# The seam between two programs of a sandwich network: spreads over four PSUM banks, first rows placed in SBUF, products without a reader

## The chip, the core and the metric

One core of a Trainium2 chip runs one program; the metric is its device time in microseconds (us). A core has five engines with instruction queues of their own: PE (TensorE: matrix products into PSUM banks), DVE (VectorE), ACT (ScalarE), POOL (GpSimd) and SP (SyncE, which here only issues transfers). They meet through semaphores alone. The kernel before was run three times: 1757.78, 1751.74 and 1754.74 us, median 1754.74.

## The reference, cut to what matters

```python
x = x + layernorm(attention(layernorm(x)))        # 32 batches x 256 steps x 128, 16 heads
x = x + layernorm(ternary_ffn(layernorm(x)))      # 128 -> 512 -> 512 -> 512 -> 128, two gelu layers
x = x + layernorm(rnn(layernorm(x)))              # h = tanh(x_t Wi + b + h Wh), over the steps, all batches at once
x = x + layernorm(shared(x') + routed(x'))        # x' = layernorm(x); one of 32 experts for each row
```

The attention works on one batch at a time. All that follows works on steps: the recurrence wants all 32 batches of a step together.

## The kernel before, in words

The program has two halves with a seam between them. `attention_layer` makes x1 = x + layernorm(attention) for each of the B = 32 batches and writes it to a tensor in DRAM, `x1_d`, ordered by step, then batch. `mixing_experts` reads `x1_d` in 16 chunks of 512 rows; chunk c holds steps 16c to 16c+15 of all batches. Each half is a block: a Python function per engine writes its instruction list by hand, a barrier of all engines ends the block, POOL clears the semaphores of that half, and the next block begins.

Attention is a pipeline over batches. `rounds` calls `step(b, f, n, m, z, y, par)` for b = -3 to 33: b is the batch whose scores are taken, z = b-1 the one whose output is finished, y = b-2 the one whose residual is made. The last two rounds have little left in them: round 32 finishes batch 31 (z) and makes the residual of batch 30 (y), round 33 makes the residual of batch 31. The chain of the finishing batch goes so:

- DVE `reciprocal` (L799 to L808) takes one over the softmax sums and splits it into `rec_parts`.
- PE `spread_out(z, g)` (L530), for g = 0 to 3, spreads a quarter of the reciprocals over the partitions: two products of 256 columns into the one PSUM bank `spread`. It waits until DVE has read the bank for g-1 (semaphore onT).
- DVE `normalise` (L817) multiplies four heads of `onT` by the bank; in the round of batch z, the statistics of batch y (L742, L746) stand between the third and the fourth.
- PE `output` (L544), eight pieces of two 128x128 products in full fp32, each pair of pieces after its `normalise`; ACT copies the result to `y_sb` (L734); DVE takes statistics (L742, L746), POOL the root (L354, L356), DVE normalises (L948) and adds the residual input `xr` into `x1` (L954).
- SP, per batch y: wait for x1 of y-1, load `xr` (L268); wait for x1 of y, store it to `x1_d` (L271). There is one buffer for each of `xr` and `x1`. At its end SP waits for all 32 stores.

`mixing_experts` begins with 15 small constants on POOL (L1190 to L1199); PE, ACT and DVE wait for all of them. SP loads chunk 0 of `x1_d` into `x1c` (L1148), DVE takes its statistics (L1736, L1740), POOL the roots (L1212, L1214), DVE normalises (L1745), PE turns the chunk (`turn4`, L1279), ACT and DVE split it, and four rounds of the first feed-forward layer follow: six products of 512 columns on PE (L1435 to L1438), tanh on ACT (L1663), two multiplications on DVE (L1944, L1950); each round of PE waits for the DVE of the round before. From the second chunk on PE has the second layer and later stages of earlier chunks to fill its waits.

`keep_busy` is already there in the end of this half: products of a weight with a weight, 128x512, into a bank nobody reads (L1351).

Of the kernel before, what the change touches and what calls it, by code (L numbers as in the profile page):

```python
# [14 lines left out]
P = 128  # L15
# [76 lines left out]

def attention_layer(nc, x, w_qk, w_v, w_rot, w_out, bonus0, bonus_step, x1_d, mix, mix_d, room, row_buf, sorted_d):

    with ExitStack() as ctx:
# [87 lines left out]
        yn = sb("yn", [P, TT, D])  # L183
        x1 = sb("x1", [P, TT, D])

# [24 lines left out]
        block = ctx.enter_context(nc.Block(no_gpsimd_drain=True))  # L210

        def rounds(eng, step):

            def row(b):
                return [v if 0 <= v < B else None for v in (b, b + 1, b + 2, b + 3, b - 1, b - 2)] + [b % 2]
            for b in range(-3, 3):
                step(*row(b))  # L220
            with eng.Fori(0, (B - 6) // 2) as i:
                for k in range(2):
                    b = 2 * i + (3 + k)
                    step(b, b + 1, b + 2, b + 3, b - 1, b - 2, 1 - k)
            for b in range(B - 3, B + 2):
                step(*row(b))

        @block.sync
        def _(sp):
# [22 lines left out]
            def step(b, f, n, m, z, y, par):  # L252
# [213 lines left out]
        def _(pe):  # L466
# [53 lines left out]
            def spread_out(z, g):  # L520
# [5 lines left out]
                if g == 0:  # L526
                    wait(pe, s["rec_parts"], z + 1)
                wait(pe, s["onT"], GROUPS * z + g)
                for i in range(2):
                    m = pe.matmul(spread[:, i, :], back_to_r[:, 2 * g + i].rearrange("p i d -> p (i d)"),  # L530
                                  rec_parts[:], start=True, stop=True)
                m.then_inc(s["p_bc"], 1)

            def output(z, par, pieces):
# [38 lines left out]
            def step(b, f, n, m, z, y, par):  # L573
# [26 lines left out]

                values(f, par, 1)
                spread_out(z, 0)
                if f is not None:
# [47 lines left out]

            rounds(pe, step)

        @block.scalar
        def _(act):
# [79 lines left out]

            rounds(act, step)

        @block.vector
        def _(dve):
# [71 lines left out]
            def normalise(z, par, g):  # L811
# [156 lines left out]

def mixing_experts(nc, early, x1_d, mix, wgu, row_buf, sorted_d, gate_up, down, sh_gate_up, sh_down, out):

# [5 lines left out]
    with ExitStack() as ctx:  # L976
# [105 lines left out]

        ctx.callback(clear, nc, list(s.values()))
        block = ctx.enter_context(nc.Block(no_gpsimd_drain=True))

        def rounds(eng, step, drain):
# [48 lines left out]
        def _(sp):  # L1135
# [140 lines left out]
        def _(pe):  # L1276
# [5 lines left out]
            def rnn_step(r, t):  # L1282
# [4 lines left out]
                          skip_group_check=True).then_inc(s["p_step"], 1)  # L1287

            pe.wait_ge(s["const"], N_CONST)

# [45 lines left out]
            def ranks(q, bank):  # L1336
# [10 lines left out]
                m_.then_inc(s["p_rank"], 1)  # L1347

            def keep_busy(n, bank):
                for _ in range(n):  # L1350
                    pe.matmul(bank[:, :], w1_part[0][:, 0:P], w1_part[0][:, :], start=True, stop=True)  # L1351

# [378 lines left out]
        def _(dve):  # L1731
# [156 lines left out]
            def step(p, a, c, v, h, q, z, par):  # L1888
# [29 lines left out]
                def first_norm():  # L1918
                    if p is not None:
                        wait(dve, s[f"xc{par}"], 8 * (p - par) + 16)  # L1920
                        stats("f", lambda k: x1c[:, k, :], p)

                if v is not None:
                    sums(v)
                if a is not None:
                    wait(dve, s["p_xn2T"], a)
                    apply("f", xn2, lambda k: x1c[:, k, :], "xn2", a)
                if v is not None:
# [106 lines left out]
def build(nc, t, out):  # L2035
# [6 lines left out]
    with ExitStack() as ctx:  # L2042
        def sb(name, shape, dt=F32):
            return ctx.enter_context(nc.sbuf_tensor(name, shape, dt))

        wgu = sb("wgu", [P, E, 2 * I])
        row_buf = [sb(f"row_buf{i}", [P, CT, ROW]) for i in range(3)]
        with ExitStack() as early:
            mix = mixing_weights(nc, ctx, early)
            attention_layer(nc, t["x"], t["w_qk"], t["w_v"], t["w_rot"], t["w_out"], t["bonus0"], t["bonus1"], x1_d,  # L2050
                            mix, t, wgu[:].rearrange("p e i -> p (e i)"), row_buf[0], sorted_d)
            mixing_experts(nc, early, x1_d, mix, wgu, row_buf, sorted_d, t["gate_up"], t["down"], t["sh_gate_up"],
                           t["sh_down"], out)

# [51 lines left out]
```

## Time and profile before

| | us |
|---|---|
| median of three runs | 1754.74 |
| the profiled execution, whole | 1755.85 |
| its span, first to last instruction | 1754.1 |
| PE busy | 1642.4 (94%) |
| DVE busy | 1317.4 (75%) |
| last attention product to first product after the seam | 766.5 to 779.9 |

The profile is of one execution. Times in its rows are microseconds from the start of the span. A row of the timeline is a run of equal instructions of one engine: start, length, engine, source line, operation, out<-in, count, and in brackets how long the engine had stood idle before it and what ended that. PEclk is the clock granted to PE: 1.00 is 2.4 GHz, 0.50 is 1.2 GHz; a value between them is a stretch with both.

### The profile page before, as it was taken

Reading aid. Unit: us, or ns where it says so; the run is one execution under the profiler, and the core shown is the slowest. Engines: PE = TensorE matmul, PEld = TensorE weight load, DVE = VectorE, ACT = ScalarE, POOL = GpSimd, SP = SyncE. Lnnn points to the kernel's source line nnn. Section 1 sums busy time; section 2 is a strip of 40 time slices with the busy share of each in tenths; the row PEclk is TensorE's granted clock in tenths of the full one; section 3 lists DMA queues with packets and bytes.
Section 4 is the critical chain, followed back from the end, with each engine's and each line's share of the span. In section 5 each row is a group of like instructions: output and inputs, shape, how many; then the busy total and the mean of one; then the engine's idle time right before and its main releaser. Section 6 shows DMA issues by size and latency. Waiting matters only on the chain.

```text
span 1754.1 us, 47186 instructions
## 1 busy us (share of the span) xinstructions
PE 1642.4 (94%) x14905; PEld 1229.3 (70%) x14905; DVE 1317.4 (75%) x3869; ACT 888.7 (51%) x2003; POOL 1000.0 (57%) x1782
## 2 busy tenths in 40 slices
PE   4999999999999999959999999999999999989996
PEld 3677777777777777537778888878787887655553
DVE  5688888888888888645567777777777775858886
ACT  3666666666666666514444444444444443224443
POOL 7888888888888888712233333333333334227777
PEclk8999999999999999869999999999999999999998
DMA  1011111111111113010120000000000001634441
GB/s 43 11 57 55 54 54 49 51 47 47 49 54 54 54 54 105 14 37 16 52 78 22 29 26 29 31 26 29 26 29 30 30 25 49 209 127 130 138 128 41
DMA packets 78259, 95.96 MB, mean 55 GB/s; under 512 B 7046, under 2 KB 62995, under 8 KB 78160
## 3 DMA queue, kind: packets, MB, share of 16 engines
q1 hardware_dynamic: 70992, 77.91, 14.1%
q0 software_dynamic: 7168, 16.87, 2.7%
q8 instruction: 46, 0.75, 0.2%
q14 instruction: 53, 0.43, 0.1%
HBM read 53.14 MB, written 43.69 MB: 55 GB/s over the span
## 4 chain that ended last, share of the span: by engine, by line
PE 40%; DVE 8%; issue 4%; POOL 2%; ACT 1%; DMA 0%; DVEq 0%; POOLq 0%; SPq 0%; ACTq 0%
PE main L1371 6%; PE main L1373 5%; PE main L1380 5%; PE main L1536 3%; PE yp L1451 3%; PE xi L1286 2%; PE main L1311 2%; PE main L1435 2%; PE main L1324 2%; PE main L1438 1%; PE main L1436 1%; PE route L1550 1%; PE xi L1550 1%; POOL out L1269 1%; PE turn L1279 1%
## 5 line engine op out<-in xcount | busy, mean ns | idle before, releaser
L662 ACT ACTIVATE wgu<-score 128x384 f32<-128x384 f32 x512 | 223.2, 490 | 80.8 <-PE score L484 79.4
L1371 PE MATMUL main<-hT_high,h_high 128*128 128x512 f32 x512 | 221.2, 432 | 0.9 <-ACT hT_high L1636 0.9
L1373 PE MATMUL main<-hT_high,h_low 128*128 128x512 f32 x512 | 201.3, 393 | 0.0
L506 PE MATMUL outp<-wgu 128*32 128x256 f32 (+1 forms) x4096 | 196.1, 333 | 1.9 <-POOL wgu L327 0.8
L327 POOL TENSOR_SCALAR_AFFINE_SELECT wgu<-wgu 128x512 f32<-128x512 f32 x256 | 165.8, 653 | 50.0 <-ACT wgu L662 32.6
L506 PEld LDWEIGHTS outp<-wgu 128*32 128x32 f32 x4096 | 116.4, 111 | 68.2 <-issue 23.5
L1380 PE MATMUL main<-hT_low,h_high 128*128 128x512 f32 x512 | 138.2, 391 | 0.1
L1944 DVE SCALAR_TENSOR_TENSOR th<-th,main 128x512 f32<-128x512 f32 x64 | 43.9, 685 | 114.5 <-ACT th L1663 114.5
L544 PE MATMUL back<-wout,wgu 128*128 128x128 f32 x1024 | 128.5, 280 | 0.0
L544 PEld LDWEIGHTS back<-wout,wgu 128*128 128x128 f32 x1024 | 121.7, 195 | 0.4
L1269 POOL DMA_INDIRECT out<-res,idx x96 | 96.5, 1005 | 44.4 <-issue 40.9
L1286 PEld LDWEIGHTS xi<-state,wh_sb 128*128 128x128 f32 x512 | 90.5, 189 | 37.1 <-ACT state L1585 20.9
L1585 ACT ACTIVATE state<-xi,bias 128x32 f32<-128x32 f32 x256 | 73.0, 285 | 79.3 <-PE xi L1286 78.6
L1380 PEld LDWEIGHTS main<-hT_low,h_high 128*128 128x128 f32 x512 | 96.1, 188 | 21.9 <-DVE hT_low L1898 0.8
L514 PE MATMUL total<-wgu,pick 128*32 128x256 f32 (+1 forms) x2048 | 108.2, 329 | 0.0
L1212 POOL TENSOR_SCALAR bve_f<-bmv_f 128x4 f32<-128x4 f32 x16 | 7.7, 482 | 175.2 <-DVE bmv_f L1740 175.2
L1627 ACT ACTIVATE hT_high<-main,sc 128x512 fp32r<-128x512 f32 x64 | 44.0, 687 | 124.1 <-PE main L1380 124.1
L1371 PEld LDWEIGHTS main<-hT_high,h_high 128*128 128x128 f32 x512 | 97.0, 189 | 13.6 <-ACT hT_high L1636 1.3
L1207 POOL TENSOR_TENSOR hT_low<-wgu,hT_high 128x512 fp32r<-128x512 f32 x64 | 82.7, 1294 | 41.2 <-ACT wgu L1628 41.0
L1373 PEld LDWEIGHTS main<-hT_high,h_low 128*128 128x128 f32 x512 | 97.1, 190 | 11.7 <-issue 0.2
L1536 PE MATMUL main<-wgu,xgT 128*128 x192 | 100.2, 604 | 3.3 <-DVE hid_g L1998 2.1
L680 ACT ACTIVATE wgu<-back 128x512 f32<-128x512 f32 x128 | 76.5, 597 | 50.3 <-PE back L559 47.0
(301 smaller groups left out, 4351.4 us busy)
## 6 DMA issues: line engine op xcount, KB each, us to landing
sorted_d<-row_buf SPq DMA_DIRECT2D x26, 772.0 KB, 3.7
xg<-sorted_d SPq DMA_DIRECT2D x48, 386.0 KB
wgu<-in_gate_up SPq DMA_DIRECT2D x4, 2048.0 KB, 8.8
xa<-in_x SPq DMA_DIRECT2D x32, 128.0 KB, 3.5
xr<-in_x SPq DMA_DIRECT2D x32, 128.0 KB, 3.2
x_d<-x SPq DMA_DIRECT2D x32, 128.0 KB, 1.9
x1c<-x_d SPq DMA_DIRECT2D x16, 256.0 KB, 2.7
x1v<-x_d SPq DMA_DIRECT2D x16, 256.0 KB, 2.7
```

What stands on the lines that cost most here:

```text
L327: pool.affine_select(out=blocks, in_=blocks, compare_op=ALU.is_ge, fill=0.0, base=0, pattern=[[0, 4], [1, P]], channel_multiplier=-1).then ...
L506: m = pe.matmul(outp[AUG * j:AUG * (j + 1), p % 2, k * P:T], val[par][:, k, h, v:v + AUG], weights(h, k), start=(k == 0), stop=(k == 1), t ...
L514: m = pe.matmul(total[AUG * j:AUG * (j + 1), k * P:T], pick[:, g, :], weights(GH * g + j, k), start=(g == 0 and k == 0), stop=(g == GROUPS ...
L544: m = pe.matmul(back[:, i * P:(i + 1) * P], onT[1 - par][:, c, i * P:(i + 1) * P], wout[:, c, :], start=(c == 0 and i == 0), stop=(c == PA ...
L662: act.activation(prob[:, h // 2 % (RING // 2), :, h % 2, :], score[h % BANKS][:, 0:SC].rearrange("p (c q) -> p c q", q=P), ACT.Exp).then_i ...
L1207: pool.tensor_tensor(hT_part[1][1][:, m, :], hT[1][:, m, :], hT_part[1][0][:, m, :].bitcast(F32), ALU.subtract).then_inc(s["h2_low"], 1)
L1269: pool.indirect_dma_start(out=out_rows[:, :], out_offset=bass.IndirectOffsetOnAxis(ap=idx[k][:, n:n + 1], axis=0), in_=res[k][:, n, :], in ...
L1286: pe.matmul(xi[:, o:o + B], wh_sb[:], state[:, prev:prev + B], start=False, stop=(t == STEPS - 1), skip_group_check=True).then_inc(s["p_st ...
L1371: pe.matmul(main[m % 2][:, :], w[0][:, k, m * P:(m + 1) * P], src[0][:, k, :], start=(k == 0), stop=False)
L1373: pe.matmul(main[m % 2][:, :], w[1][:, k, m * P:(m + 1) * P], src[0][:, k, :], start=False, stop=False)
L1380: mm = pe.matmul(main[m % 2][:, :], w[0][:, k, m * P:(m + 1) * P], src[1][:, k, :], start=False, stop=(k == HC - 1))
L1536: pe.matmul(main[2 * (r % 2) + i][:, :], xgT[r % 2][:, i * P:(i + 1) * P], wgu[:, bass.ds(e, 1), :].rearrange("p o i -> p (o i)"), start=T ...
```

## The change

Three things, all at the seam:

- In round 32 the four spreads of the last batch go to four banks (`spread`, the two score banks and `front`), so that none waits for DVE to have read the one before. Only the first has the wait.
- Chunk 0 is no longer loaded from DRAM in the second half. Its rows are put into a third row buffer in SBUF, `first_rows`, in the first half: SP waits until batch 30 is stored, then issues four transfers from `x1_d`, one for each of the four groups of 32 partitions: 31 partitions (batches 0 to 30), four rows of 512 bytes on each. The rows of the last batch go from `x1`, SBUF to SBUF, in four transfers of 4 partitions (two issued by SP, two by ACT). SP no longer waits for the last store; the second half waits for it before the load of chunk 1. DVE waits for the eight transfers before the statistics of chunk 0. The tile `x1` now lies in the second row buffer.
- PE gets products without a reader: 13 in round 32 ahead of the first spread, 18 at the end of its first list, 14 at the start of its second, ahead of the wait for the constants.

```diff
-        x1 = sb("x1", [P, TT, D])
+        row_buf, first_rows = row_bufs[0], row_bufs[2]
+        x1 = row_bufs[1][:, 0:TT, 0:D]
...
+        def spread_bank(z, g):
+            if isinstance(z, int) and z == B - 1:
+                return (spread, *(bank[:, :].rearrange("p (i t) -> p i t", i=2) for bank in (*score, front)))[g]
+            return spread
...
+        first_steps = x1_d[0:CHUNK // B].rearrange("(k u) b d -> u b k d", u=P // B)
+
+        def last_rows(eng, k):
+            u = P // B
+            eng.dma_start(first_rows[B - 1:P:B, k, 0:D], x1[k * u:(k + 1) * u, 0, :]).then_inc(seam["first_rows"], 16)
...
+                    last = isinstance(y, int) and y == B - 1
+                    if last:
+                        sp.wait_ge(s["x1_out"], 16 * (B - 1))
+                        for u in range(P // B):
+                            sp.dma_start(first_rows[u * B:(u + 1) * B - 1, :, 0:D],
+                                         first_steps[u, 0:B - 1]).then_inc(seam["first_rows"], 16)
                     wait(sp, s["x1"], y + 1)
+                    if last:
+                        last_rows(sp, 0)
+                        last_rows(sp, 1)
                     sp.dma_start(x1_d[:, y, :].rearrange("(i p) d -> p i d", p=P) if isinstance(y, int)
                                  else x1_d[:, bass.ds(y, 1), :].rearrange("(i p) o d -> p (i o) d", p=P),
-                                 x1[:]).then_inc(s["x1_out"], 16)
+                                 x1[:]).then_inc(seam["last_out"] if last else s["x1_out"], 16)
 
             rounds(sp, step)
-            sp.wait_ge(s["x1_out"], 16 * B)
...
-                wait(pe, s["onT"], GROUPS * z + g)
+                if not isinstance(z, int) or z < B - 1 or g == 0:
+                    wait(pe, s["onT"], GROUPS * z + g)
+                bank = spread_bank(z, g)
...
+                if isinstance(z, int) and z == B - 1:
+                    pe.wait_ge(s["mix_split_v"], 2)
+                    keep_busy(13)
                 spread_out(z, 0)
...
             rounds(pe, step)
+            keep_busy(18)
...
             rounds(act, step)
+            act.wait_ge(s["x1"], B)
+            last_rows(act, 2)
+            last_rows(act, 3)
...
-                dve.tensor_tensor(o, spread[:], o, ALU.mult).then_inc(s["onT"], 1)
+                dve.tensor_tensor(o, spread_bank(z, g)[:, :, :], o, ALU.mult).then_inc(s["onT"], 1)
...
-                if p is not None:
+                if isinstance(p, int) and p == 1:
+                    sp.wait_ge(seam["last_out"], 16)
+                elif p is not None:
                     wait(sp, s["xn2"], p)
+                if p is not None and not (isinstance(p, int) and p == 0):
                     sp.dma_start(x1c[:], chunk_of(x1_rows, p)).then_inc(s[f"xc{par}"], 16)
...
+            keep_busy(14, main[3])
             pe.wait_ge(s["const"], N_CONST)
...
-                        wait(dve, s[f"xc{par}"], 8 * (p - par) + 16)
-                        stats("f", lambda k: x1c[:, k, :], p)
+                        if isinstance(p, int) and p == 0:
+                            dve.wait_ge(seam["first_rows"], 16 * (P // B + CT))
+                        else:
+                            wait(dve, s[f"xc{par}"], 8 * (p - par) + 16 * par)
+                        stats("f", lambda k: input_rows(p, k), p)
```

## Rows read from the trace of the kernel before

**Rows 1.** The page's slices of the span, PE's granted clock in tenths.
```profile
PEclk8999999999999999869999999999999999999998
```
**Rows 2.** Stretches around the seam: busy us (count) by engine, PEclk, DMA share, GB/s.
```profile
750.00:755.00 5.00, 2.21 (x50) 1.37 (x48) 2.62 (x4) 0.98 (x2) 0.00 (x0) 1.00 0.18 50
755.00:760.00 5.00, 1.85 (x7) 0.42 (x8) 2.86 (x6) 0.00 (x0) 0.00 (x0) 0.51 0.00 0
785.00:790.00 5.00, 3.17 (x7) 2.06 (x8) 2.44 (x4) 1.21 (x2) 0.00 (x0) 0.57 0.00 0
```
**Rows 3.** Timeline of PE, the last batches' spreads and output products.
```profile
746.39 3.74 PE L544 MATMUL back<-wout,wgu 128*128 128x128 f32 x32
...
755.79 0.61 PE L530 MATMUL spread<-rec_parts,back_to_r 128*128 128x256 bf16 x2 [3.58 <-DVE rec_parts L808]
...
760.37 6.13 PE L544 MATMUL back<-wout,wgu 128*128 128x128 f32 x32
```
**Rows 4.** Timeline of DVE over the same stretch, to chunk 0.
```profile
759.22 0.69 DVE L817 TENSOR_TENSOR wgu<-spread,wgu 128x512 f32<-128x512 f32 x1 [0.70 <-PE spread L530]
759.83 0.47 DVE L742 BATCH_NORM_STATS2 stat_y<-y_sb 128x6 f32<-128x128 f32 x2
...
760.61 0.69 DVE L817 TENSOR_TENSOR wgu<-spread,wgu 128x512 f32<-128x512 f32 x1
...
762.34 0.43 DVE L954 TENSOR_TENSOR x<-yn,xr 128x256 f32<-128x256 f32 x1
...
769.45 0.43 DVE L954 TENSOR_TENSOR x<-yn,xr 128x256 f32<-128x256 f32 x1
...
775.88 0.87 DVE L1736 BATCH_NORM_STATS2 bstat_f<-x1c 128x6 f32<-128x128 f32 x4 [6.00 <-DMA x1c<-x_d]
```
**Rows 5.** Timeline of SP's queue: start, and length of the issue alone.
```profile
762.79 0.38 SPq L271 DMA_DIRECT2D x_d<-x  x1
763.22 0.47 SPq L268 DMA_DIRECT2D xr<-in_x  x1
769.90 0.38 SPq L271 DMA_DIRECT2D x_d<-x  x1
773.02 7.15 SPq L1148 DMA_DIRECT2D x1c<-x_d  x2
```
**Rows 6.** Issues of 763.0 to 765.5 us: size, us from issue to landing.
```profile
x_d<-x SPq DMA_DIRECT2D x1, 128.0 KB, 1.9
xr<-in_x SPq DMA_DIRECT2D x1, 128.0 KB, 2.2
```
**Rows 7.** Timeline of POOL, the last of the second half's constants.
```profile
775.52 0.10 POOL L1199 MEMSET eps<- 128x1 f32 x1
```
**Rows 8.** Transfers, 773.9 to 775.7 us: busy tenths in 40 slices, packets, share of 16 engines.
```profile
DMA  0001339593576677899999999953322221100000
...
DMA packets 528, 0.26 MB, mean 146 GB/s; under 512 B 16, under 2 KB 528, under 8 KB 528
...
q1 hardware_dynamic: 528, 0.26, 52.2%
```
**Rows 9.** Line 1161, four large loads: length of the issue in ns (min/median/max), landing.
```profile
L1161 SPq DMA_DIRECT2D wd<-in_down x4: 3107/3418/9007, 1489.7 to 1506.9; - x4
...
DMA to landing us min/median/max: 10.3/13.5/16.9
```
**Rows 10.** Timeline of PE: chunk 0's turn and first layer; products without a reader.
```profile
779.92 1.09 PE L1279 MATMUL turn<-ident,xn 128*128 128x128 f32 x4 [13.42 <-DVE xn L1745]
...
785.76 0.79 PE L1435 MATMUL main<-xn2T_high,w_high 128*128 128x512 f32 x1 [1.07 <-DVE wgu L1950]
...
789.76 0.49 PE L1435 MATMUL main<-xn2T_high,w_high 128*128 128x512 f32 x1 [1.07 <-DVE wgu L1950]
...
793.08 0.50 PE L1435 MATMUL main<-xn2T_high,w_high 128*128 128x512 f32 x1 [1.66 <-DVE wgu L1950]
...
1539.85 8.45 PE L1351 MATMUL xi<-w_high 128*128 128x512 f32 x36
```

More of the change, by code:

```diff
@@ L90, in mixing_weights, with attention_layer @@
     return mix
-def attention_layer(nc, x, w_qk, w_v, w_rot, w_out, bonus0, bonus_step, x1_d, mix, mix_d, room, row_buf, sorted_d):
+def attention_layer(nc, x, w_qk, w_v, w_rot, w_out, bonus0, bonus_step, x1_d, mix, mix_d, room, row_bufs, sorted_d, seam):
     with ExitStack() as ctx:
@@ L527, in spread_out, with keep_busy @@
                     wait(pe, s["rec_parts"], z + 1)
-                wait(pe, s["onT"], GROUPS * z + g)
+                if not isinstance(z, int) or z < B - 1 or g == 0:
+                    wait(pe, s["onT"], GROUPS * z + g)
+                bank = spread_bank(z, g)
                 for i in range(2):
-                    m = pe.matmul(spread[:, i, :], back_to_r[:, 2 * g + i].rearrange("p i d -> p (i d)"),
+                    m = pe.matmul(bank[:, i, :], back_to_r[:, 2 * g + i].rearrange("p i d -> p (i d)"),
                                   rec_parts[:], start=True, stop=True)
                 m.then_inc(s["p_bc"], 1)
+            def keep_busy(n):
+                for _ in range(n):
+                    pe.matmul(turned[:, :], mix["w1"][0][:, 0:P], mix["w1"][0][:, :], start=True, stop=True)
             def output(z, par, pieces):
@@ L966, in part, with mixing_experts @@
     return t[:, i * n:(i + 1) * n] if isinstance(i, int) else t[:, bass.ds(i * n, n)]
-def mixing_experts(nc, early, x1_d, mix, wgu, row_buf, sorted_d, gate_up, down, sh_gate_up, sh_down, out):
+def mixing_experts(nc, early, x1_d, mix, wgu, row_buf, sorted_d, gate_up, down, sh_gate_up, sh_down, out, seam):
     with ExitStack() as ctx:
@@ L1081, in mixing_experts, with input_rows @@
         PAGE = 20
-        ctx.callback(clear, nc, list(s.values()))
+        ctx.callback(clear, nc, list(s.values()) + list(seam.values()))
         block = ctx.enter_context(nc.Block(no_gpsimd_drain=True))
+        def input_rows(c, k):
+            return (row_buf[2][:, k, 0:D] if isinstance(c, int) and c == 0 else x1c[:, k, :])
         def rounds(eng, step, drain):
@@ L1287, in rnn_step, with keep_busy @@
                           skip_group_check=True).then_inc(s["p_step"], 1)
+            def keep_busy(n, bank):
+                for _ in range(n):
+                    pe.matmul(bank[:, :], w1_part[0][:, 0:P], w1_part[0][:, :], start=True, stop=True)
+            keep_busy(14, main[3])
             pe.wait_ge(s["const"], N_CONST)
@@ L1347, in ranks @@
                 m_.then_inc(s["p_rank"], 1)
-            def keep_busy(n, bank):
-                for _ in range(n):
-                    pe.matmul(bank[:, :], w1_part[0][:, 0:P], w1_part[0][:, :], start=True, stop=True)
             def state_turn(v):
@@ L1926, in step @@
                     wait(dve, s["p_xn2T"], a)
[L1927 removed]
+                    apply("f", xn2, lambda k: input_rows(a, k), "xn2", a)
                 if v is not None:
@@ L2044, in sb @@
             return ctx.enter_context(nc.sbuf_tensor(name, shape, dt))
+        seam = {name: ctx.enter_context(nc.semaphore("seam_" + name)) for name in ("last_out", "first_rows")}
         wgu = sb("wgu", [P, E, 2 * I])
@@ L2050, in build @@
             attention_layer(nc, t["x"], t["w_qk"], t["w_v"], t["w_rot"], t["w_out"], t["bonus0"], t["bonus1"], x1_d,
-                            mix, t, wgu[:].rearrange("p e i -> p (e i)"), row_buf[0], sorted_d)
+                            mix, t, wgu[:].rearrange("p e i -> p (e i)"), row_buf, sorted_d, seam)
             mixing_experts(nc, early, x1_d, mix, wgu, row_buf, sorted_d, t["gate_up"], t["down"], t["sh_gate_up"],
-                           t["sh_down"], out)
+                           t["sh_down"], out, seam)
 def host_layout(np, i):
```

## The prediction, made blind

> **What bounds the kernel now.** I read four views in this order. The page's slices show PE near its full clock everywhere but at the start, in two slices just before the middle and at the end [rows 1]; those two slices are the seam. The stretches there show why: from 755 to 760 us PE works 1.85 of 5 us at a clock of 0.51 and DVE 2.86, nobody is full, so a chain of waits rules [rows 2]. PE's timeline shows the chain of the last batch: 3.58 us without work, then four spreads one after the other, then 32 output products that take 6.13 us where the same 32 took 3.74 one batch earlier [rows 3]. DVE's shows the other half of the ping-pong (0.70 us of waiting and 0.69 of work a quarter, 1.39 together), then x1 of batch 31 at 769.45 to 769.88, then 6.00 us of waiting for chunk 0 until 775.88 [rows 4]. After it come 4.04 us of norm until PE's turn at 779.92, and the rounds of the first layer, 4.00 us each at the low clock and 3.32 at the high one [rows 10]. Nothing runs beside this, so what DVE's start at 775.88 moves, the end moves by. I measure each step against that time. The profiled execution took 1755.85 us (1754.1 of span, 1.75 around it), the median of three is 1754.74, 1.11 less; the sum is made against the first, and the difference is laid on the second.
>
> **Spreads in four banks, 13 products.** Thirteen products of 512 columns cost 8.45/36 = 0.235 us each [rows 10], 3.1 us, inside PE's 3.58 us of waiting [rows 3]: nothing is late through them while the clock is 1.00, as it is up to 755 [rows 2]; at half of it they would take 6.1 us and be 2.5 late. The low clock came after that idle stretch; with PE busy I take 1.00. The first spread stays at 755.8. DVE's first product can start at 756.2; the next follow at 0.61 (759.22 to 759.83 [rows 4]): 756.8 and 757.4. The statistics of batch 30 take 0.78 (759.83 to 760.61), so the fourth runs 758.8 to 759.5, 1.8 earlier than at 760.61. x1 of batch 30 moves by the same 1.8: from 762.34 to 760.55, ready at 761.0. The output needs 3.74/4 = 0.94 a pair of pieces: 757.0 on, its last pair not before 759.5 and after the third at 759.8, so it ends at 760.7 instead of 760.37 + 6.13 = 766.5: 5.8 earlier. x1 of batch 31 started 2.95 after that end, now 763.7; `xr` for it is issued behind the store of batch 30 at 761.45 and lands 2.2 later [rows 5, 6], 763.65, a near tie. x1 is ready at 764.1 instead of 769.88: 5.8 gained, if nothing else is late.
>
> **What is late next: the transfers of chunk 0.** They can't be issued before batch 30's store has landed: 761.0 + 1.9 = 762.9 [rows 6]. Four issues at 0.38 to 0.47 [rows 5] end near 764.7. A transfer begins to move about 1.0 after its issue (773.02, first busy slices at 774.0) [rows 5, 8], so the first packet moves at 763.9. The packets number 4 x 31 x 4 = 496 of 512 bytes. The like load of chunk 0 had 528 packets and took 52.2% of 16 engines over 1.8 us, 15.0 us of engine time, 28.5 ns each [rows 8]. It had 16 packets under 512 bytes beside its 512: one small one an engine, so it lay on all 16, eight partitions each. No row shows a transfer of 31 partitions. The two ends: on 16 engines, 496 x 28.5/16 = 0.9 us, landed by 766, of no effect; on one, 14.1 us, done at 778.0. They are far apart. The nearest rows show only transfers cut into 16 equal shares of whole partitions, and 31, a prime, has no equal share but one of all 31; I take the one engine. All four then queue on the same one if each starts its shares at the same engine, as the 16-way ones give no sign against. The last batch's sixteen rows wait behind them, 0.1 us at most; DVE began 0.35 after the last packet of chunk 0's load (775.5 by the slices [rows 8], 775.88), so now at 778.4: **2.5 later than 775.88**, not 6 earlier.
>
> On this the Trainium skill speaks against the change: "DMA: Bandwidth & Descriptors", "Why a DMA increments its semaphore by 16 and not by 1", says a transfer is cut along its outermost dimension over the largest count up to 16 that divides it on both sides, 100 partitions giving 10 engines and 127 one. By it 31 gives one; no row here shows it.
>
> **SP and ACT at the end of the first half.** SP no longer waits for the last landing (769.90 + 1.9 = 771.8, and 1.2 more to the first instruction of the second half at 773.02 [rows 5]). It issues three transfers after x1, 1.2 us, and the four before; ACT issues two in a queue with nothing behind. With free issues SP ends at 765.9 and the second half begins at 767.1. But issues are held when too much waits: the four loads of line 1161, 2048 rows of 512 bytes each, took 3.1 to 9.0 us to issue; the last was issued from 1506.9 to 1510.0 and landed 10.3 after its start, 7.2 after the issue's end, some two transfers of 3.4 us. So about two, 256 rows an engine, may wait [rows 9]. Of mine 248 may then wait, the fourth is taken at 763.9 + 248 x 0.0285 = 771.0, three more end at 772.2, and the second half begins at 773.4. Its constants end 2.6 later (775.62 - 773.02 [rows 5, 7]), 776.0: before 778.4 still, so hidden by the transfer.
>
> **18 and 14 products.** 18 x 0.235 = 4.2 us from 760.7 to 764.9, before SP is done; at the low clock 8.5, to 769.2, still hidden by SP's 772. 14 take 3.3 us (6.6 at the low clock) from 773.4, done by 780.0; the turn is due at 778.4 + 4.04 = 782.4. They delay nothing. Do they bring the clock? Before the turn PE stands 2.4 to 5.7 us idle; a wait of 3.58 was followed by the low clock [rows 2, 3]. I count 0 to -2.5 and take 0 (the whole prize would be 0.5 in the turn and three rounds at 4.00 - 3.32, 2.5 us [rows 10]).
>
> The skill weighs in here too: "TensorE: Matmul & The Clock Gate", "HAM oscillation — how this bites in real kernels", says that a wait between bursts lets the clock fall and the next burst starts slow. By it the 14 products help only if the wait behind them is short.
>
> Second-half loads: chunk 1's is needed some 20 us later, and the clearing of two more semaphores is a few tenths at most. 0.
>
> **Sum.** +2.5: 1755.85 + 2.5 = 1758.35 for the profiled execution, 1754.74 + 2.5 = **1757.2** for the median. The likeliest case's own range: packets a fifth quicker (their busy times may overlap) give 763.9 + 11.3, start at 775.7, -0.2; SP held until only one transfer waits (774.5, then 1.2, 1.2, 2.6: 779.6) +3.7; with the clock's 2.5 either way 1752 to 1761.
>
> **Rivals.**
> - *The transfers are spread over the engines*: landed by 766. Then DVE waits for the constants: second half at 767.1, constants at 769.7, DVE at 769.8, 6.1 earlier: **1748.6**. For it: every transfer seen is on 16 engines. Against: none of them has an indivisible count. Chance 0.17.
> - *The same, and the clock stays up through chunk 0's first layer*: 2.5 more, **1746.1**. Against it, a gap of 3 us is left ahead of the turn. 0.05.
> - *Slower: SP is held until every packet has gone.* If the queue of one engine takes nothing ahead, SP ends only at 778.0 + 1.2, the second half begins at 780.4, constants and DVE at 783.1: +7.2, **1762**. It decides from the point where fewer than about 160 packets may wait; rows 9 speak for 256. 0.07.
> - *The first batch of products runs at half clock and sets the end* (13: 2.5 late, output 6.13 long): x1 some 5 us later, hidden behind 778.4; it adds nothing to the forecast and would bring the first rival back to about 1754.
>
> Forecast 0.66; 0.05 is left for a split over a few engines (two: 7 us less transfer, then the block's end rules, 1751).
>
> **Chances.** 0.3% of the time, 5.3 us, is about what a measurement of this kernel can tell from no change. Faster by more: most of the first rival, which lies only 0.9 beyond the bound, and all of the second: 0.17. Slower by more: the third and the forecast's upper tail, 0.12. Within: 0.71. The range that leaves two in ten out runs from 1749 to 1761.
>
> **What would show it.** Right: DVE's first statistics near 778, ended by a landing; a DMA share near 1/16 for 14 us from 764; SP's fourth issue of many us; output products in 3.7 us ending near 760.7; no idle ahead of the last batch's second to fourth spread. Wrong: a DMA share near 0.9 for 1 us, statistics near 770 behind the constants.

## The result, and the profile after

The changed kernel took 1761.47 us (median of 22 runs, 1758.57 to 1764.41), the kernel before 1754.92 beside it (22 runs, 1751.74 to 1760.22). The ratio is 1.0031, interval 1.0023 to 1.0039, some 5.4 us more. The forecast said 1757.2 within 1749 to 1761 and gave 0.71 to a change within 0.3%. The time lies half a microsecond above the range, and the interval straddles the 0.3%; laid on the forecast's own base, 1754.74 times 1.0031 is 1760.2. The medians are 6.6 us apart and not 5.4: the executions of the kernel before lie in two groups, 13 from 1751.7 to 1755.1 and 9 from 1757.8 to 1760.2, and its median depends on how many fall into each. The profiled execution took 1762.56 us, 1760.8 of them span.

The first view is the timeline of the changed kernel around the seam (start, busy us, engine, line, operation; in brackets the idle time before and its releaser).

```profile
753.41 3.26 PE L558 MATMUL turned<-w_high 128*128 128x512 f32 x13
...
757.06 0.39 PE L552 MATMUL spread<-rec_parts,back_to_r 128*128 128x256 bf16 x2 [0.39 <-DVE rec_parts L841]
...
758.32 3.81 PE L570 MATMUL back<-wout,wgu 128*128 128x128 f32 x32 [0.22 <-DVE wgu L850]
...
761.79 0.43 DVE L987 TENSOR_TENSOR row_buf<-yn,xr 128x256 f32<-128x256 f32 x1
...
764.14 8.22 SPq L286 DMA_DIRECT2D row_buf<-x_d  x4
765.08 0.42 DVE L987 TENSOR_TENSOR row_buf<-yn,xr 128x256 f32<-128x256 f32 x1
765.54 1.64 ACTq L238 DMA_DIRECT2D row_buf<-row_buf  x2
772.40 3.71 SPq L238 DMA_DIRECT2D row_buf<-row_buf  x2
776.57 0.42 SPq L292 DMA_DIRECT2D x_d<-row_buf  x1
778.29 0.10 POOL L1229 MEMSET first_mark<- 128x1 f32 x1 [13.88 <-POOLq L65]
...
780.79 0.10 POOL L1238 MEMSET eps<- 128x1 f32 x1
780.93 0.87 DVE L1776 BATCH_NORM_STATS2 bstat_f<-row_buf 128x6 f32<-128x128 f32 x4 [15.42 <-POOL eps L1238]
```

What the reader is to see: the first five rows are as fast as was hoped. The gap of 3.58 us without work is filled but for 0.39, the four spreads run without a wait, the output products take 3.81 us instead of 6.13, and x1 of the last batch starts at 765.08 instead of 769.45 [rows 3, 4]. Then DVE waits 15.42 us, and the releaser isn't a landing but POOL's `eps`, the last constant of the second half. The second half began at 778.29 instead of 773.02 [rows 5], 1.30 us after SP's last issue had ended at 776.99. SP sat in seven issues from 764.14 on.

Two executions are seldom in step: this one was already 1.27 us late at 751, before anything changed (ACT's copy of batch 30's y starts at 751.43 here and at 750.16 in the kernel before). So all seams below are measured from that copy to PE's turn: 779.92 - 750.16 = 29.76 us in the kernel before, 784.98 - 751.43 = 33.55 in the changed one, **3.8 more**. A second profile of the kernel before (e11 below) gave 29.79.

```profile
784.98 0.63 PE L1318 MATMUL turn<-ident,xn 128*128 128x128 f32 x4 [0.65 <-DVE xn L1785]
```

The stretches of the same kernel (columns as in [rows 2]) show what the queue did meanwhile:

```profile
765.00:770.00 5.00, 1.25 (x6) 0.71 (x4) 0.47 (x2) 0.00 (x0) 0.00 (x0) 1.00 0.07 19
770.00:775.00 5.00, 0.00 (x0) 0.00 (x0) 0.00 (x0) 0.00 (x0) 0.00 (x0) 0.52 0.07 19
775.00:780.00 5.00, 1.67 (x4) 1.43 (x5) 0.00 (x0) 0.00 (x0) 1.18 (x10) 0.50 0.15 42
```

A DMA share of 0.07 at 19 GB/s is one engine of sixteen, for ten us and more: 150 packets of 512 bytes in four us, 26.7 ns each. The stream isn't without gaps. It stood still for 0.2 us at 765.5 and for 0.4 at 765.9; the packets from 766.0 to 766.5:

```profile
DMA packets 8, 0.00 MB, mean 8 GB/s; under 512 B 0, under 2 KB 8, under 8 KB 8
```

The issues of SP one by one (line, count, ns min/median/max, first and last start):

```profile
L286 SPq DMA_DIRECT2D row_buf<-x_d x1: 301/301/301, 764.1 to 764.1; - x1
...
L286 SPq DMA_DIRECT2D row_buf<-x_d x2: 687/2188/3688, 764.5 to 765.2; - x2
...
L286 SPq DMA_DIRECT2D row_buf<-x_d x2: 3407/3548/3688, 765.2 to 769.0; - x2
...
L238 SPq DMA_DIRECT2D row_buf<-row_buf x1: 3144/3144/3144, 772.4 to 772.4; - x1
```

The first two are free (0.30 and 0.69 us). The third takes 3.69, the fourth 3.41, and the first transfer of the last batch's rows, four packets in all, takes 3.14. The first packet moved at 765.05, 0.9 after its issue. When the three long issues end (768.91, 772.36, 775.55), 137, 264 and 383 packets have moved, counted one by one in the trace. Ahead of their own packets there then remain 248 - 137 = 111, 372 - 264 = 108 and 496 - 383 = 113. So an issue ends once about 110 packets are left ahead of it on that engine. (The second, short issue ended with 119 ahead.)

### The profile page after: what moved, and what is told of

Its sections match the earlier page's. It is cut to its first block, busy times and chain, and to the rows that moved or that the text cites. A ratio compares the mean times of both kernels' runs of the same rounds, so it can differ in the third digit from the quotient of the medians.

```text
span 1760.8 us, 47288 instructions
## 1 busy us (share of the span) xinstructions
PE 1654.2 (94%) x14950; PEld 1238.8 (70%) x14950; DVE 1316.3 (75%) x3869; ACT 888.8 (50%) x2003; POOL 1000.3 (57%) x1782
## 4 chain that ended last, share of the span: by engine, by line
PE 40%; DVE 8%; issue 4%; POOL 2%; ACT 1%; DMA 0%; DVEq 0%; POOLq 0%; SPq 0%; ACTq 0%
PE main L1411 6%; PE main L1413 5%; PE main L1420 5%; PE main L1576 4%; PE yp L1491 3%; PE xi L1325 2%; PE main L1355 2%; PE main L1475 2%; PE main L1368 2%; PE main L1478 1%; PE main L1476 1%; PE route L1590 1%; PE xi L1590 1%; PE yp L1598 1%; POOL out L1308 1%
```

## The experiments

The theory: the 31-partition transfers lie on one DMA engine, SP's issues are held behind them, and the second half, whose constants come last, starts late. The rivals: products and clock, the landing itself, or the time of x1. All kernels were timed in five rounds against the kernel before, whose medians in the three sessions were 1756.0, 1757.2 and 1757.0. So the ratio is what is to be compared, not the median. The seam is the one defined above.

| kernel | median us | ratio to before (95%) | seam us, less 29.76 |
|---|---|---|---|
| changed | 1761.47 | 1.0031 (1.0023, 1.0039) | +3.8 |
| e1 transfers of 16 and 15 | 1754.42 | 0.9986 (0.9975, 0.9997) | -3.3 |
| e2 half of them | 1755.94 | 0.9997 (0.9985, 1.0009) | -0.3 |
| e3 chunk 0 read back | 1752.23 | 0.9975 (0.9964, 0.9987) | -5.8 |
| e4 no products | 1762.36 | 1.0030 (1.0021, 1.0040) | +4.0 |
| e5 transfers of 30, earlier | 1752.35 | 0.9970 (0.9960, 0.9981) | -5.1 |
| e6 banks alone | 1754.72 | 0.9980 (0.9968, 0.9992) | -5.0 |
| e7 tail on ACT | 1763.03 | 1.0030 (1.0020, 1.0040) | +3.1 |
| e8 rows alone | 1764.13 | 1.0037 (1.0023, 1.0051) | +5.8 |
| e9 = e5, early statistics | 1750.39 | 0.9960 (0.9947, 0.9972) | -6.6 |
| e10 = e3, early statistics | 1751.81 | 0.9966 (0.9954, 0.9978) | -5.7 |
| e11 kernel before again | 1757.76 | 1.0001 (0.9991, 1.0011) | 0.0 |
| e12 eight transfers | 1763.41 | 1.0031 (1.0019, 1.0043) | +3.7 |

**e1: the shape of the transfers.**

```
                         for u in range(P // B):
-                            sp.dma_start(first_rows[u * B:(u + 1) * B - 1, :, 0:D],
-                                         first_steps[u, 0:B - 1]).then_inc(seam["first_rows"], 16)
+                            for lo, hi in ((0, 16), (16, B - 1)):
+                                sp.dma_start(first_rows[u * B + lo:u * B + hi, :, 0:D],
+                                             first_steps[u, lo:hi]).then_inc(seam["first_rows"], 16)
...
```

Here and below, DVE's wait counts as many transfers as are issued; that line is left out.

> Each transfer of 31 partitions is replaced by two, of 16 and of 15 partitions (eight issues, the same 496 packets); all else is the changed kernel. Theory (31 partitions lie on one DMA engine and SP's issues are held until only some hundred packets wait): the rows move at once over 15 or 16 engines and land before 769; SP issues eight at about 0.4 us, 762.7 to 766.3, the two row transfers and the store by 768.0, the second half begins at 769.3, DVE's statistics at 771.9, nine us before the 780.9 of the changed kernel: about 1752.5 against 1761.5 for the changed kernel and 1754.9 for the kernel before. Rival (products and their clock phases cost the time, the transfers were only a bystander): within 2 us of 1761. Rival (eight issues queue for as long as four): second half still at 778, 1761.

Timeline of e1, SP and what follows it:

```profile
765.04 4.00 SPq L287 DMA_DIRECT2D row_buf<-x_d  x8
...
769.09 1.24 SPq L238 DMA_DIRECT2D row_buf<-row_buf  x2
770.36 0.44 SPq L293 DMA_DIRECT2D x_d<-row_buf  x1
772.10 0.10 POOL L1230 MEMSET first_mark<- 128x1 f32 x1 [6.78 <-POOLq L65]
...
774.75 0.87 DVE L1777 BATCH_NORM_STATS2 bstat_f<-row_buf 128x6 f32<-128x128 f32 x4 [8.34 <-POOL eps L1239]
```

Eight issues with the same 496 packets take 4.00 us where four took 8.22, and the seam is 7.1 us shorter than the changed kernel's. That is the theory's way, if less than its nine. The expectation had put the first issue at 762.7, which is the forecast's time, beside the 780.9 of the changed kernel's trace, where the first issue stands at 764.14: 1.4 of the missing 1.9. Eight free issues cost 0.50 us each where it had 0.45, which is most of the rest. By the ratios the time fell by some 8 us against the changed kernel.

**e2: half the dose.** The same edit for u = 2 and 3 alone.

> Only half of the dose: the first two transfers stay at 31 partitions (248 packets), the last two are cut into 16 and 15. Theory: 248 packets of 26.7 ns on one engine from 765, so 6.6 us, landed at 771.7; SP is held until some hundred of them wait, to about 769, and ends its other issues at 771.5; the second half begins near 772.9, DVE's statistics at 775.5, 5.4 before the changed kernel: about 1756. The rival of the forecast (two transfers may wait freely, 256 packets): SP is not held, second half at 769.3, DVE at 772: 1752.5, as with all four cut. If the transfers have nothing to do with it: 1761.

The third issue of e2, a transfer of 16 partitions with only four packets on each engine, behind two of 31:

```profile
L287 SPq DMA_DIRECT2D row_buf<-x_d x1: 4156/4156/4156, 762.6 to 762.6; - x1
```

248 packets on one engine hold the next issue for 4.16 us, however small it is, until 112 are left; the three behind it took 0.4 each. That falls against the reading of the forecast, by which two transfers may wait freely. The seam was 4.1 us below the changed kernel's, where 5.4 were expected, and the time near the expected one.

**e3: chunk 0 read back, banks and products kept**; **e6: banks alone**; **e4: everything but the products.** e6 is the kernel before with these lines, e3 with the three groups of products besides:

```
-                wait(pe, s["onT"], GROUPS * z + g)
+                if not isinstance(z, int) or z < B - 1 or g == 0:
+                    wait(pe, s["onT"], GROUPS * z + g)
+                bank = spread_bank(z, g)
...
-                dve.tensor_tensor(o, spread[:], o, ALU.mult).then_inc(s["onT"], 1)
+                dve.tensor_tensor(o, spread_bank(z, g)[:, :, :], o, ALU.mult).then_inc(s["onT"], 1)
```

and e4 is the changed kernel less

```
-                    keep_busy(13)
...
-            keep_busy(18)
...
-            keep_busy(14, main[3])
```

> The kernel before with the four PSUM banks and all three groups of products, chunk 0 read back from HBM as before. Theory: x1 of the last batch is ready 5.8 us earlier and all that follows with it (store, its landing, second half, load, DVE's statistics near 770): 1749, six below the kernel before. Rival (14 products at half clock hold PE's turn, or the clock falls in another place and takes it back): 1752 to 1755.

> The kernel before with the four PSUM banks alone: no products, chunk 0 read back. Theory: of the 5.8 us that banks and products gave together, the output products at the low clock take 0.9 to 2.4 back (4.7 us instead of 3.8 as in the changed kernel without products): from the copy to the statistics 21 to 22 us against 19.9 with the products; with chunk 0's first layer at the low clock for a while longer, 1753.5 against 1752.2. Rival (the products are worth nothing or cost the turn something): 1752 or less.

> The changed kernel without any of its 13, 18 and 14 products. Theory: the output products run at the low clock again, 6.1 instead of 3.8 us, x1 of the last batch is ready 2 to 3 us later, at 767 to 768, but SP's fourth issue starts only at 769, so nothing moves: 1761.5 within 1 us, DVE's statistics near 781. If the 14 products hold the turn or cost clock later (they ran at 0.43 us each): 1 to 3 us faster than the changed kernel. If the products keep a clock that matters: 1763 or more.

Timeline of e3:

```profile
765.28 0.42 DVE L969 TENSOR_TENSOR x<-yn,xr 128x256 f32<-128x256 f32 x1
765.73 0.38 SPq L276 DMA_DIRECT2D x_d<-x  x1
768.85 6.96 SPq L1163 DMA_DIRECT2D x1c<-x_d  x2
768.85 0.10 POOL L1205 MEMSET first_mark<- 128x1 f32 x1 [4.28 <-POOLq L65]
768.89 3.45 PE L1306 MATMUL main<-w_high 128*128 128x512 f32 x14 [2.50 <-PEq L65]
771.37 0.10 POOL L1214 MEMSET eps<- 128x1 f32 x1
771.50 0.88 DVE L1752 BATCH_NORM_STATS2 bstat_f<-x1c 128x6 f32<-128x128 f32 x4 [5.80 <-POOL eps L1214]
```

The seam of e3 is 23.97 us, 5.8 below the kernel before, exactly what the forecast took for x1. In time it brought 4.4 us (0.25%). And DVE waits for `eps`, not for the chunk: reading it back is hidden by the constants, if barely (with that wait moved, in e10 below, the landing came 2.7 us after the second half's start, where the constants take 2.6). So the rows on chip had nothing to save, and their price came on top. e6 holds 5.0 of the 5.8, so the banks carry it, and the products bring 0.8 in the seam. In time the two can't be told apart (0.9980 and 0.9975, intervals overlapping). e4 shows the clock's part. PE's output products there, without the 13 ahead of them:

```profile
756.51 4.74 PE L570 MATMUL back<-wout,wgu 128*128 128x128 f32 x32
```

That is 4.74 us against 3.81, and x1 of the last batch comes 1.2 us later after the copy (764.20 - 749.33 against 765.08 - 751.43). Yet the seam is that of the changed kernel within 0.3: the held issues hide it.

**e8: the rows alone** (the kernel before with the rows placed on chip, one bank, no products).

> The kernel before with only the rows placed on chip (31 partitions a transfer), one bank, no products. Theory: the chain from the store of batch 30 on is the same, and that store comes 1.8 us later than with four banks: from the copy to the statistics 31.2 us against 29.5 with banks and products, though x1 of the last batch comes almost 6 us later; 1763 to 1764, nine above the kernel before. Rival (x1 of the last batch decides, and the held issues only by chance end near it): 6 us over the changed kernel, 1767.

```profile
782.09 0.87 DVE L1773 BATCH_NORM_STATS2 bstat_f<-row_buf 128x6 f32<-128x128 f32 x4 [12.94 <-POOL eps L1236]
```

The statistics came 31.5 us after the copy (at 750.62), as expected. x1 of the last batch came 4.5 us later after the copy than in the changed kernel (768.73 - 750.62 against 765.08 - 751.43), the statistics only 2.0 later. The store of batch 30, issued 1.6 us later here, sets them, not the last x1.

**e7: the tail taken off SP.** This builds what the prediction had assumed: SP held by its four transfers alone.

```
-                    if last:
-                        last_rows(sp, 0)
-                        last_rows(sp, 1)
...
+            for k in range(CT):
+                last_rows(act, k)
+            act.dma_start(x1_d[:, B - 1, :].rearrange("(i p) d -> p i d", p=P), x1[:]).then_inc(seam["last_out"], 16)
```

> The changed kernel with the four transfers of 31 partitions where they are, but everything that stood behind them on SP (two row transfers, the last store) issued by ACT. Theory: SP is held only by its fourth issue, until the second transfer has passed, so it is free at 772.4 instead of 777.0 and the constants are ready at 776.4; then the landing of the one-engine transfers ends last, at 778.3 to 778.6, which is what the prediction on record had said of the change itself. From the copy to the statistics 27.2 us against 29.5: 1759, 2.3 below the changed kernel and 3 above the kernel before. Rival (the hold is the engine's, not the queue's: ACT's transfers are held as well): ACT ends at 777 as SP did, 1761.5. Rival (the landing is not what ends last once SP is free, because the packets had been delayed by the hold): 1757.

```profile
763.00 9.06 SPq L286 DMA_DIRECT2D row_buf<-x_d  x4
...
764.43 2.72 ACTq L238 DMA_DIRECT2D row_buf<-row_buf  x4
767.19 0.87 ACTq L768 DMA_DIRECT2D x_d<-row_buf  x1
773.70 1.46 SPq L1186 DMA_DIRECT2D x1c<-x_d  x1
773.71 0.10 POOL L1228 MEMSET first_mark<- 128x1 f32 x1 [10.44 <-POOLq L65]
...
775.22 0.80 SPq L1188 DMA_DIRECT2D sgu<-in_sh_gate_up  x1
...
776.22 0.10 POOL L1237 MEMSET eps<- 128x1 f32 x1
779.10 0.87 DVE L1775 BATCH_NORM_STATS2 bstat_f<-row_buf 128x6 f32<-128x128 f32 x4 [14.70 <-DMA row_buf<-x_d]
```

ACT's five issues ran free (2.72 and 0.87 us, 764.4 to 768.1) while SP's third was held (764.1 to 768.2): the hold is the queue's. Their packets did share the DMA engine, for ACT's store landed 5.0 us after its issue, where 1.9 is usual [rows 6]. The second half starts 773.71 - 750.28 = 23.4 us after the copy, against 26.9 in the changed kernel, the constants are ready at 776.2, and now the releaser of DVE is the landing, as the forecast said. But it ends 28.8 us after the copy instead of 27.2. The first packet moved at 763.9; at 26.7 ns each 366 would have moved by 773.7, when the second half issues its first load, and 327 had. So 1.0 us was lost before any of these loads, most of it in a pause at the start. The packets from 764 to 765 us, where the two microseconds behind it have 42 and 40 on this queue:

```profile
DMA packets 6, 0.00 MB, mean 3 GB/s; under 512 B 0, under 2 KB 6, under 8 KB 6
```

The 169 packets left at 773.7 need 4.5 us, to 778.2, and DVE starts at 779.10: 0.9 later for landing, start and whatever the loads took. (Before the change DVE began 0.35 after the last packet.) What makes the pauses no run shows. The gain of 2.3 us that was expected is not in the time: the ratio's interval, 3.5 to 7.0 us above the kernel before, leaves out the expected 3 and holds the changed kernel's 5.4. In the seam 0.7 is left of it. What e7 shows is the releaser and SP's earlier end.

**e12: smaller pieces on the same engine.**

```
                         for u in range(P // B):
-                            sp.dma_start(first_rows[u * B:(u + 1) * B - 1, :, 0:D],
-                                         first_steps[u, 0:B - 1]).then_inc(seam["first_rows"], 16)
+                            for k in range(0, CT, 2):
+                                sp.dma_start(first_rows[u * B:(u + 1) * B - 1, k:k + 2, 0:D],
+                                             first_steps[u, 0:B - 1, k:k + 2]).then_inc(seam["first_rows"], 16)
```

> The changed kernel with each transfer of 31 partitions cut in two along the four rows of a partition: eight transfers of 62 packets, all still on the one engine. Theory (a queue takes about 248 packets of one engine ahead, and the room of a transfer comes back when that transfer is over): four issues are free, the fifth to eighth each wait for one of 1.65 us, the first row transfer for the fifth to be over, 1.6 us earlier than now; SP ends 1.6 us earlier, from the copy to the statistics 27.9 us against 29.5, 1760. If two transfers may be ahead, whatever their size: SP's first row transfer is held until the seventh is over, 31 us, 1763. If the room is counted by packets as they go: 29.5, as now.

```profile
L287 SPq DMA_DIRECT2D row_buf<-x_d x1: 1935/1935/1935, 766.9 to 766.9; - x1
...
L287 SPq DMA_DIRECT2D row_buf<-x_d x2: 1661/1798/1935, 766.9 to 768.8; - x2
...
L287 SPq DMA_DIRECT2D row_buf<-x_d x2: 1654/1658/1661, 768.8 to 770.5; - x2
```

My theory of a room of 248 packets fell here. The fourth issue was held already, with 186 packets issued ahead of it, and the seam stayed at +3.7 as the third option had it. The fourth, fifth and sixth issues end (768.8, 770.5, 772.2) with 115, 111 and 111 packets ahead of their own, the ones behind them with 108 and 109, as in the changed kernel, whether a transfer has 124 packets or 62. One thing e12 doesn't separate: whether the room comes back packet by packet or when a transfer is over. With pieces of 124 and of 62 a transfer always ends with 124 left ahead, and the held issues of the changed kernel and of e12 ended 0.2 to 0.4 us after such an end. Only e7 has a case that parts the two: there the stream paused 0.46 us at 771.2, right behind such an end, and SP's fourth issue ended 0.8 us after it, again with 108 packets ahead. That speaks for the packets, by one issue.

**e5: thirty partitions, one batch earlier.**

```
+                    if isinstance(y, int) and y == B - 2:
+                        sp.wait_ge(s["x1_out"], 16 * (B - 2))
+                        for u in range(P // B):
+                            sp.dma_start(first_rows[u * B:(u + 1) * B - 2, :, 0:D],
+                                         first_steps[u, 0:B - 2]).then_inc(seam["first_rows"], 16)
...
-                        for u in range(P // B):
-                            sp.dma_start(first_rows[u * B:(u + 1) * B - 1, :, 0:D],
-                                         first_steps[u, 0:B - 1]).then_inc(seam["first_rows"], 16)
+                        sp.dma_start(first_rows[B - 2:P:B, :, 0:D], first_steps[:, B - 2]).then_inc(seam["first_rows"], 16)
```

> The changed kernel with the rows of batches 0 to 29 loaded in four transfers of 30 partitions, issued one batch earlier (behind the landing of batch 29's store), batch 30's sixteen rows in one more transfer, batch 31's on chip as before. Theory (the one-engine transfers and the issues held behind them are the whole loss): after x1 of the last batch SP issues only two row transfers and the store, 1.7 us; the second half begins 3.0 us after x1 is ready, DVE's statistics 2.7 later. From the copy of batch 30's y to the statistics 19.5 us (25.7 in the kernel before, 29.5 in the changed one, 19.9 with chunk 0 read back): 1752, 9.5 below the changed kernel and as fast as the version with the read back. Rival (30 partitions lie on few engines or one as well): the statistics come when 480 packets have passed, but they start ten us earlier, so the statistics would still be near; then SP's last rows are held by some us, 22 us and 1755. If placing rows on chip gains more than the constants allow: 1750.

The four transfers of 30 weren't held (2.79 us of issues together). From the copy to the statistics it took 20.6 us, one more than expected: x1 of the last batch was ready 14.4 us after the copy where 13.8 had been taken, and the second half began 3.6 after it and not 3.0, the two row transfers costing SP 1.54 us. The seam is 5.1 below the kernel before, and the version with the read back is as good. DVE again waited for `eps` (6.27 us).

**e9 and e10: the cover taken away.** DVE's wait for the constants put behind its first statistics, in e5 and in e3:

```
-            dve.wait_ge(s["const"], N_CONST)
...
                         stats("f", lambda k: input_rows(p, k), p)
+                        if isinstance(p, int) and p == 0:
+                            dve.wait_ge(s["const"], N_CONST)
```

> The version with transfers of 30 partitions, and DVE's wait for the second half's constants put behind its first statistics, which read none of them. Theory (on-chip rows are hidden by POOL's 2.5 us of constants, and worth something once DVE need not wait for them): DVE's statistics start when the last rows land, 0.3 to 0.7 us after the second half begins instead of 2.6, and PE's turn 5.2 us after it instead of 6.7, since POOL's root now follows the constants at once; 1.5 us below the version with 30 partitions, ratio to before 0.996. Rival (another wait of the norm is behind the constants): no change.

> The same move of DVE's wait in the version that reads chunk 0 back. Theory: the read back takes 2.6 us from the second half's start, as long as the constants, so the statistics start 2.6 to 3.0 us after it as before, the turn 6.7, and the time stays that of the version with the read back, ratio 0.9975. If it gains 1 us or more, the landing was earlier than I take it.

Timeline of e9, then of e10:

```profile
767.59 0.10 POOL L1232 MEMSET first_mark<- 128x1 f32 x1 [4.77 <-POOLq L65]
...
767.63 0.87 DVE L1777 BATCH_NORM_STATS2 bstat_f<-row_buf 128x6 f32<-128x128 f32 x4 [3.70 <-PEq L65]
...
770.10 0.10 POOL L1241 MEMSET eps<- 128x1 f32 x1
...
772.96 0.63 PE L1321 MATMUL turn<-ident,xn 128*128 128x128 f32 x4 [0.30 <-DVE xn L1786]
```

```profile
765.98 0.10 POOL L1205 MEMSET first_mark<- 128x1 f32 x1 [4.29 <-POOLq L65]
768.49 0.10 POOL L1214 MEMSET eps<- 128x1 f32 x1
768.67 0.87 DVE L1750 BATCH_NORM_STATS2 bstat_f<-x1c 128x6 f32<-128x128 f32 x4 [5.84 <-DMA x1c<-x_d]
...
772.80 1.08 PE L1294 MATMUL turn<-ident,xn 128*128 128x128 f32 x4 [3.33 <-DVE xn L1759]
```

With the rows on chip the statistics start 0.04 us after the second half, the turn 5.37 after it, and the seam is 1.5 shorter than in e5. With the read back they start 2.69 after it, now released by the landing, and the turn comes 6.82 after it, as before the move (6.70). So rows on chip are worth 1.0 us of seam here, once DVE needn't wait. e9 is the fastest, 7.0 us (0.40%) below the kernel before and 12.4 below the changed one; its lead on e10 lies within the intervals.

**e11: the kernel before, timed against itself.**

> The kernel before, unchanged, timed against itself: ratio 1.000 within 0.001, and a second profile of it. From the copy of batch 30's y to the statistics 25.7 us as in the first profile if that one is typical; all seam differences named so far rest on it. If it is 24.5 or less, the excess of about 1 us that most comparisons show over their seam difference is explained by it.

The ratio is 1.0001 and its seam 29.79 us: the reference of all comparisons holds. The two profiled executions of this one kernel differ by 3.9 us (1755.85 and 1759.74), and all of it lies outside the seam: 2.0 ahead of the copy (750.16 and 752.17), 1.8 between PE's turn and the end of the span (974.2 and 976.0).

## Why the prediction was wrong on the size and right on the way

Times of the changed kernel are moved back by its 1.27 us here, to stand beside the forecast's.

- *Spreads, 13 products, clock*: right. First spread at 755.8 (forecast 755.8), output ended 760.9 (760.7), x1 of batch 30 ready at 761.0 (761.0), of the last at 764.2 (764.1). PE's granted clock was 1.00 up to 770. The rival of half-clock products didn't come.
- *One engine for 31 partitions*: right. The first packet moved at 763.8 (forecast 763.9) and the 496th at 777.3 (778.0), one packet took 26.7 ns instead of 28.5, and 16, 15 and 30 partitions behaved otherwise (e1, e5). By the rule of the Trainium skill, "DMA: Bandwidth & Descriptors", "Why a DMA increments its semaphore by 16 and not by 1", this was to be expected, and the trace agrees: a DMA share of 0.07, one in sixteen.
- *SP's fourth issue taken at 771.0*: 771.1, in part by luck. It ended with 264 packets moved and not 248, each of 26.7 ns and not 28.5, and the two errors cancel. That the third issue would be held as well (3.69 us) follows from the forecast's rule, but it didn't say so.
- *"Three more end at 772.2, and the second half begins at 773.4"*: **this step failed**. SP ended at 775.7, and the second half began at 777.0. From [rows 9] I had read that two transfers, 256 packets an engine, may wait. But the 7.2 us between the end of the last issue and its landing hold that transfer's own 128 packets too, so only about 128 were ahead of it. I used the number rightly for the fourth transfer, which is large, and forgot it for the small one behind: at 771.1 there were some 230 packets ahead of that one, and it was held 3.14 us, until 113 were left. This is the case that the forecast's own range had named (SP held until only one transfer waits, +3.7); it came to +3.8 in the seam.
- *The landing sets the end*: wrong for that reason. The constants came last, DVE's start at 779.7 instead of 778.4. Where SP was freed (e7), the landing did rule, 28.8 us after the copy, where the forecast had 778.4 - 750.2 = 28.2.
- *The slower rival* (SP held until every packet has gone; "It decides from the point where fewer than about 160 packets may wait"): its place was the right one and its threshold was passed, since about 110 may wait. Its price of 7.2 was too high for the seam, because the last issues needed the queue down to 110, not empty.
- *The range*: "with the clock's 2.5 either way 1752 to 1761" isn't what its terms add up to. From 1757.2, -0.2 and -2.5 give 1754.5, and +3.7 gives 1760.9, or 1763.4 with 2.5 of clock on top. The case that came true used up the whole upper side by itself, and nothing was left there for the scatter between executions.
- *18 and 14 products*: they delayed nothing, as said. The 14 took 6.00 us, most of it at the low level, and the turn 0.65 us behind them took 0.63 us instead of 1.09. The rounds after it still came 3.90 to 4.00 us apart, so no more of the forecast's 2.5 us of clock came. But that is one execution. In e12 PE had stood idle as long (11.99 us) and the 14 took as long (6.16), and the rounds came 3.65, 3.33 and 3.32 apart. Granted clock from 790 to 795 in the changed kernel, then in e12 (the last three columns are PEclk, DMA share and GB/s):

```profile
790.00:795.00 5.00, 3.66 (x8) 2.46 (x9) 2.25 (x4) 1.20 (x2) 0.00 (x0) 0.50 0.00 0
```

```profile
790.00:795.00 5.00, 2.00 (x7) 1.35 (x8) 3.01 (x5) 1.21 (x2) 0.00 (x0) 1.00 0.00 0
```

- Nor does the idle time ahead of the 14 settle how they run: 3.45 us at the high level behind 2.50 and 3.20 us of it (e3, e5), but 5.03 behind 2.98 (e9) and 4.79 behind 8.65 (e7). What they bring stays open. "TensorE: Matmul & The Clock Gate", "HAM oscillation — how this bites in real kernels", in the Trainium skill has it that a wait between bursts lets the clock fall; the granted 0.52 and 0.50 of 770 to 780, where PE waits, agree.
- *What stays open*: of the 5.4 us in the ratio, 3.8 are seen in the seam, and the other 1.6 are not explained. Over all comparisons the time exceeds the seam difference by -0.4 to +2.2 us, 0.8 on average, each but the changed kernel's and e7's within its interval. No trace places the excess: the changed kernel's copy at 751.43 and its 975.8 us behind the turn both lie between those of the two executions of the kernel before (e11). Behind the turn alone one execution differs from another by up to 3.7 us (973.7 in e1, 977.4 in e7), in part with the clock of chunk 0's first layer: from the turn to the second layer's first product the changed kernel took 14.8 us and e12 13.2, the kernel before 14.7 and 15.4. So it may be chance, but no run shows it to be.

## What to carry to other kernels

Before a transfer is made of an awkward number of partitions such as 31, look at what count it can be cut into (here 30, and 16 and 15, did well), and then at everything that is issued behind it on the same queue: a four-packet transfer waited almost as long as a large one (3.14 us against 3.41). When reading how far a queue runs ahead from the time between an issue's end and its landing, take off the transfer's own packets. And before work is moved to bring an input earlier, see which wait ends last there: here the constants hid the read back, and one moved wait (e9) was what made the input worth having early. And a single profile doesn't tell what products without a reader do to the clock: the same kernel's rounds differed from one execution to the next.

## What the runs showed of the hardware that I had not expected

- An issue on SP's queue is held until about 110 packets of 512 bytes are left ahead of its own on the engine it needs: 108 to 113 in the changed kernel, 112 in e2, 108 to 115 in e12, with 124 or 62 packets of its own there or a single one. That packets count and not ended transfers rests on one issue of e7. ACT's queue wasn't held by SP's packets on the same engine (e7).
- One engine moved 512-byte packets at 26.7 ns each, 19 GB/s, for twelve us (766.4 to 778.6). Near the start of the stream it paused, 0.2 and 0.4 us in the changed kernel and 0.9 us in e7, before the next stage had issued anything; no run shows why.
